# Capacity layer with one accumulator table in HBM instead of two

## The reference, cut to what matters

```
x = hidden.reshape(-1, 128)                    # n = 4096 tokens
topk_idx, topk_w = route(x)                    # 8 experts of 64 for each token
buf  = zeros(E, CAP+1, h).at[e, pos_c].set(x[token])[:, :CAP]
y    = (silu(buf @ w_gate) * (buf @ w_up)) @ w_down
out  = zeros((n, h)).at[token].add(y_slots * w_slot)
x    = x + out
```

## Time and profile before

| | us |
|---|---|
| median of 3 runs (range) | 2344.34 (2340.66 to 2345.98) |
| the profiled execution's own time | 2356.74 |
| its span, first to last instruction | 2355.0 |
| busy in the span: PE, DVE, POOL, ACT | 1682.6, 1580.0, 902.3, 816.1 |
| first scatter-add starts, last one starts | 2114.15, 2323.37 |
| first load of stage three starts | 2330.36 |

### The profile page before, as it was taken

How to read it: one execution, slowest core, us unless ns; L and a number is a source line. 1 busy time by engine, 2 the same in 40 slices (tenths; PEclk the granted TensorE clock), 3 DMA queues, 4 the chain that set the end, 5 groups by cost and what they waited for, 6 DMA issues and landing times. The chain is left out here.

```text
span 2355.0 us, 49069 instructions
## 1 busy us (share of the span) xinstructions
PE 1682.6 (71%) x14850; PEld 1190.1 (51%) x14853; DVE 1580.0 (67%) x3661; ACT 816.1 (35%) x1800; POOL 902.3 (38%) x1185
## 2 busy tenths in 40 slices
PE   3999943312399888995996799626998898158883
PEld 2777732011277655663785344214776677135552
DVE  4999963989767753446687899675555677763332
ACT  2544420334355422322563678400000564012221
POOL 1788810346234243014441000004554342018894
PEclk9999965555599988997998899857999898555555
DMA  3222200000000041111003477206774000214446
GB/s 110 66 65 66 63 2 26 0 0 1 7 1 0 15 153 39 41 37 33 1 0 64 180 304 304 104 0 201 284 286 153 2 0 28 86 42 78 77 78 139
DMA packets 178867, 184.55 MB, mean 78 GB/s; under 512 B 101410, under 2 KB 163682, under 8 KB 171234
## 3 DMA queue, kind: packets, MB, share of 16 engines
q1 hardware_dynamic: 155298, 114.23, 15.7%
q10 hardware_dynamic: 9152, 54.63, 6.4%
q0 software_dynamic: 14336, 14.69, 3.5%
HBM read 107.38 MB, written 72.45 MB: 76 GB/s over the span
## 5 line engine op out<-in xcount | busy, mean ns | idle before, releaser
L1920 POOL TENSOR_TENSOR gr_work<-gr_ring 128x512 f32<-128x512 f32 x96 | 121.7, 1280 | 398.3 <-DVE gr_part L1932 310.7
L748 DVE TENSOR_REDUCE at_mx<-at_psS 128x16 f32<-128x1024 f32 x96 | 117.6, 1225 | 95.3 <-PE at_psS L653 95.3
L711 ACT ACTIVATE at_ET<-at_psT 128x512 f32<-128x512 f32 x192 | 114.6, 597 | 172.0 <-PE at_psT L662 171.4
L617 POOL TENSOR_TENSOR at_KM<-at_K,at_mask 128x512 f32<-128x512 f32 x96 | 100.0, 1042 | 154.6 <-ACT at_Q L698 154.6
L1995 PEld LDWEIGHTS gr_psY<-gr_wd,gr_work 128*128 128x128 f32 x1024 | 132.0, 192 | 38.6 <-DVE gr_work L1955 23.9
L388 POOL TENSOR_TENSOR at_E<-at_Z,at_mx 128x512 f32<-128x512 f32 x128 | 130.9, 1044 | 51.2 <-DVE at_mx L513 51.2
L1995 PE MATMUL gr_psY<-gr_wd,gr_work 128*128 128x128 f32 x1024 | 139.9, 280 | 11.6 <-DVE gr_work L1955 11.6
L662 PE MATMUL at_psT<-kept_ident,at_Z 128*128 128x128 f32 x768 | 127.8, 290 | 9.1 <-DVE at_Z L761 5.0
L1844 PE MATMUL gr_psV<-kept_xT,gr_wu 128*128 (+1 forms) x256 | 126.7, 596 | 2.1 <-ACT gr_V L1698 2.1
L249 ACT ACT_TABLE_LOAD x6 | 7.7, 1283 | 346.6 <-PEq L63 331.0
L675 PE MATMUL at_psO<-at_VZ,at_ET 128*64 128x18 f32 x3072 | 107.0, 212 | 15.4 <-ACT at_ET L711 3.9
(11 more groups left out here) (562 smaller groups left out, 4700.2 us busy)
## 6 DMA issues: line engine op xcount, KB each, us to landing
gr_spill<-gr_ring SPq DMA_DIRECT2D x28, 1792.0 KB, 5.7
gr_ring<-gr_spill ACTq DMA_DIRECT2D x28, 1792.0 KB, 7.0
at_amask<-mask_Bx16xSxS_ff SPq DMA_DIRECT2D x128, 128.0 KB, 2.8
cap_acc<-cap_zero SPq DMA_DIRECT2D x2, 2112.0 KB, 12.5
cap_sums<-cap_acc SPq DMA_DIRECT2D x8, 512.0 KB, 7.3
ex_xs<-ex_zero SPq DMA_DIRECT2D x1, 2496.0 KB, 11.1
ex_row<-ex_xs SPq DMA_DIRECT2D x39, 64.0 KB, 1.8
ex_ys<-ex_out SPq DMA_DIRECT2D x39, 64.0 KB, 1.6
```

Of the source, the lines that this page charges most:

```text
L617: pool.tensor_tensor(KM[:, s, :, :], K[:, s, :].unsqueeze(1).broadcast_to([P, 4, P]), mask4[:, :].unsqueeze(2).broadcast_to([P, 4, P]), AL ...
L711: act.activation(ET[:, 4 * a:4 * a + 4, :].rearrange("p r q -> p (r q)"), psT[:, :], ACT.Exp, scale=QK_SCALE).then_inc(exped, 1)
L748: dve.tensor_reduce(mx[:, :].rearrange("p (g v) -> p g v", v=4), psS[:, :, 0:256].rearrange("p g (v k) -> p g v k", k=SEQ), AX.X, ALU.max) ...
L1920: pool.tensor_tensor(tp[:, s % 4, :], ring[:, s // 4, first, :], ring[:, s // 4, first + 1, :], ALU.mult).then_inc(pooled, 1)
```

## The change

`ACCS` goes from 2 to 1. All else follows from it: one table instead of two is allocated and zeroed, every scatter-add goes to this table, the wait ahead of a scatter-add is for the one just before it (index s - 1 instead of s - 2), and stage three loads and adds one table instead of two. The loads of stage three go from eight to four (512 KB each), DVE's additions from eight to four; `z_out` is awaited at 32 instead of 48.

```
-ACCS = 2
+ACCS = 1
...
     wait_past(pool, added[(s - ACCS) % 4], 16 * (2 * n + (s + 4 - ACCS) // 4))
     carry(1, e)
     pool.indirect_dma_start(accs[s % ACCS], ...idx2..., Y[:, s % 4, :], None,
                             compute_op=ALU.add).then_inc(added[s % 4], 16)
```

## The result

The changed kernel takes 2387.76 us (median of 4 runs, 2385.38 to 2389.92), the kernel before beside it 2345.16: a ratio of 1.0179, with a 95% interval of 1.0164 to 1.0194, or +42.6 us. Forecast were +24.7 us and 2369.0. The direction was right and the time lies at the upper edge of the range (2356 to 2389), but outside the forecast's own range (2359 to 2380).

The account below looks back on a forecast made before the run. Stage two was taken as bound by POOL's queue, stage three by the DMA engines. Loop +25.8, last four scatter-adds +6.4, stage three -7.5 gave +24.7 us: 2369.0 us, own range 2359 to 2380, wider range 2356 to 2389.

Parts of the forecast that it names:

- What bounds the loop: Stage two: POOL's queue sets the step, 3.403 us before the change and 3.84 forecast, +25.8 us over 59 steps.
- L: Stage two: time from a scatter-add's start on POOL to POOL's release by its landing, forecast 3.03 + 0.45 = 3.48 us.
- Both bounds from the trace of before: Release behind the last packet: at most 0.47 us in stage two's last scatter-adds, some 0.5 in layer 1's scatter; 0.45 taken.
- the drain: End of stage two: last four scatter-adds, no gather between; forecast 4 x 3.72 us instead of 8.44, +6.4 us.
- 0.36 is from the carry to the scatter-add: Stage two's step: time from the small POOL instruction holding the wait to the scatter-add, added to the release time.
- Stage three: Final loads, additions and stores, bound by the DMA engines: four loads and four additions fewer, forecast -7.5 us of 24.6.
- Stage one, hidden: Zeroing of the tables: one DMA of 2112 KB less, hidden by DVE's sorting, forecast 0 us.
- the 7.0 us unchanged: From the last scatter-add's start to stage three's first load: forecast to stay 7.0 us, whatever it consists of.
- Rival 1: Stage two: landing counted once the last packet is through, step stays 3.40 us, total -2.9 us, 2341.4; chance 0.07.
- rival 2: Stage two: landing completes late, step up to 6.8 us, at most +212 us, 2556; chance 0.06.
- Rival 3: Stage two: scatter-add packets collide more with weight loads, step 4.17 us, total 2388.5; chance 0.09.
- Rival 4: Stage three gives nothing, since last load, addition and store follow each other anyway: 2376.5 us; chance 0.04.

Follow-up runs that it names:

- e1: Kernel before with both tables kept, only the wait ahead of a scatter-add changed to the one just issued: 2394.89 us, ratio 1.0213.
- e2: Kernel before with its loop kept, but stage three loads and adds only the first table: 2334.58 us, ratio 0.9952.
- e5: Kernel before, two tables, with stage three moved into stage two's block, each table loaded after its own scatter-adds land: 2337.07 us, ratio 0.9969.
- e6: Changed kernel with an extra POOL instruction ahead of the carry taking the wait for Y, and stage three in stage two's block: 2366.04 us, ratio 1.0076.
- e9: Changed kernel with two tiny instructions ahead of the scatter-add, two waits each, the landing's on the first, Y's on the second: 2396.45 us, ratio 1.0211.

## Why the prediction was right or wrong

- **What bounds the loop**: right. POOL's queue set the step, and what was added to it came out in full; e1 shows that the wait alone makes the whole step.
- **L, from the scatter-add's start to the release**: right, 3.48 us forecast and 3.48 measured (the median; the mean of the 59 steps is 3.51). Both bounds from the trace of before (at most 0.47 us behind the last packet in the drain, some 0.5 in layer 1) held: about 0.5.
- **The term that was mis-sized** is "0.36 is from the carry to the scatter-add; after a real wait of POOL the same step took 2319.35 - 2319.01 = 0.34". It measures 0.67 in most steps and 0.63 in the drain. The one row that I took for the price after a stall was of a stall of 0.50 us that ended with ACT's Y, and in the compiled program the wait for Y is on that carry itself, the one for the landing ahead of it. So it was one instance, and of the cheap case. The trace of before had the dear case also, which I did not weigh: the first gather of stage two, and in earlier layers nine restarts of POOL ahead of an indirect DMA, of which seven took 0.66 us or more and two 0.42 and 0.47. One of each:

```profile
2102.36 0.20 POOL L2228 TENSOR_TENSOR cap_spare<-cap_nought 128x1 f32<-128x1 f32 x1 [5.18 <-DVE cap_idx L2272]
2103.09 1.01 POOL L2234 DMA_INDIRECT cap_GX<-cap_rows,cap_idx  x1 [0.53 <-POOL cap_spare L2228]
```
```profile
864.82 0.18 POOL L1293 TENSOR_TENSOR ex_spare<-ex_zero 128x1 f32<-128x1 f32 x1 [2.26 <-DVE ex_row L1397]
865.48 0.98 POOL L1294 DMA_INDIRECT ex_xs<-ex_row,ex_idx  x1 [0.47 <-POOL ex_spare L1293]
```

  Even the row from which I bounded L has it: the scatter-add of 2323.37 is 0.63 us behind its carry at 2322.74. I took that carry as not held. It may have been held by the landing: in e2, with the same code, it came 1.56 us behind the scatter-add ahead instead of 1.44, and 3.51 behind the one that it waits for. The cost: 59 x (4.133 - 3.84) = 17.3 us, of which 15 are the gap (mean 0.62 instead of 0.36) and 2 the mean of L; and 1.8 in the drain, 1.2 of them the gap.
- **Stage three**: right in kind (e2), low by 1.5 us: it was sized from volumes and mean rates, and the idle stretch ahead of the last store was not counted apart. With these terms 24.7 + 17.3 + 1.8 - 1.5 = 42.3.
- **Stage one, hidden; the 7.0 us unchanged**: right. From the zeroing's start to SP's first DMA of stage two it is 83.34 us in the kernel before and 83.37 in the changed one; and 7.03 us. Of the 7.0 us some 3.6 go with the change of block (e5, e6).
- **Rival 1** (release with the last packet) and **rival 2** (late completion) are refuted by the release 3.48 us behind the start. For rival 2, the Trainium skill, "DMA: Bandwidth & Descriptors", in its section on the anatomy of one DMA on the GpSimd path, has most of about 2 us as the write's receipt; here the measured 0.5 us behind the last packet decides.
- **Rival 3** (2388.5) has almost the measured time, and is wrong all the same: it has longer transfers, so a longer L. L stayed; the step grew behind the release. A time that fits does not make a mechanism right.
- **Rival 4** falls with e2.

## What to carry to other kernels

Before a wait is put on a queue that is the bound, work out three terms: when the awaited thing lands, when the release comes, and what the queue takes from the release to its next real work. The third was the one missed, and some 16 us of the loss came from it; its price is read from all restarts after a stall that the trace has, since they are not alike, and not from one. On POOL, where such a wait can't be avoided, put it on the instruction directly ahead of the indirect DMA, and all waits that are long fulfilled on an earlier one (some 20 us here). Look in the compiled program where the wait ended up, since the compiler moves waits. And where the next stage waits for landings, it can wait for them itself, in the same block.

## What the runs showed of the hardware that I had not expected

- The start of an indirect DMA on POOL behind a stall: 0.34 us after the instruction directly ahead of it when that one held the unmet wait, 0.63 to 0.68 us when the wait was on an instruction before that, 0.75 us after the release in e9.
- Leaving a block whose POOL queue ends with an indirect DMA: about 3.6 us between the landing and SP's next issue (7.0 less the 3.4 of e5 and e6), against 0.26 us in the change from stage one to two. Which part of the change takes them is not shown.
- An indirect write to HBM of 128 rows of 512 bytes is released after 2.4 us, with addition after 3.4 to 3.5; the addition also takes POOL 0.6 us more to issue.
